# Decoder layer on one core: the first sequence's first two pairs staged, turned and reduced by halves of the tokens, beside the projections

## The reference

```python
qkv = x @ w_qkv
q, k, v = split(qkv)                      # 16 heads of 16
q = q * cos + rotate_half(q) * sin        # the same for k
att = where(causal, q @ k.T * scale, min)
y = softmax(att) @ v
x = layernorm(x + y @ w_proj)
x = layernorm(x + cross_attention(x, ctx))
x = layernorm(x + ffn(x))
```

## Time and profile before

| | us |
|---|---|
| median of 3 runs | 871.85 (871.64 to 872.28) |
| the profiled execution | 867.16 |
| its span, first to last instruction | 865.4 |
| TensorE busy | 803.2 (93%) |
| VectorE busy | 479.6 (55%) |
| ScalarE busy | 376.2 (43%) |
| GpSimd busy | 321.4 (37%) |

### The profile page before, as it was taken

The page is one execution under the profiler, slowest core; times in us unless marked ns, Lnnn a source line. Parts: engine busy times, 40 slices in busy tenths (PEclk is TensorE's granted clock), DMA queues, the critical chain, the costliest instruction groups (busy, mean ns, idle before and its releaser), DMA issues.

```text
span 865.4 us, 14094 instructions
## 1 busy us (share of the span) xinstructions
PE 803.2 (93%) x5044; PEld 542.1 (63%) x5044; DVE 479.6 (55%) x1257; ACT 376.2 (43%) x768; POOL 321.4 (37%) x585
## 2 busy tenths in 40 slices
PE   8879988898998999999999888989899899999996
PEld 4544444346776777877777634433577678887886
DVE  3797878536675542155444888871477661125113
ACT  0686776773444211223212377767544432113110
POOL 6313325245312543445332424323631143335433
PEclk9957999999999999999999999999999999999999
DMA  9900534430000232434332035510000000000000
GB/s 274 411 29 33 195 119 147 149 131 1 2 2 25 73 122 74 145 116 141 109 123 73 26 123 182 227 58 2 2 1 2 2 2 1 0 7 20 1 1 26
DMA packets 24712, 68.70 MB, mean 79 GB/s; under 512 B 4449, under 2 KB 11873, under 8 KB 24417
## 3 DMA queue, kind: packets, MB, share of 16 engines
q1 hardware_dynamic: 24640, 67.77, 22.4%
HBM read 65.40 MB, written 13.63 MB: 91 GB/s over the span
## 4 chain that ended last, share of the span: by engine, by line
PE 77%; DVE 10%; ACT 8%; issue 3%; POOL 2%; POOLq 0%; ACTq 0%; DVEq 0%
PE bank_pair L906 27%; PE bank_pair L729 7%; PE bank_pair L894 6%; PE bank_pair L711 6%; ACT prob_s L1048 5%; PE bank_pair L824 4%; PE bank_pair L615 3%; PE bank_pair L761 3%; PE bank_pair L675 3%; DVE bank_pair L1236 3%; PE bank_pair L659 3%; DVE max_raw L1234 3%; PE bank_pair L836 2%; PE bank_pair L903 2%; PE bank_pair L813 2%
## 5 line engine op out<-in xcount | busy, mean ns | idle before, releaser
L1539 POOL TENSOR_TENSOR hid_lo_s<-act_raw_s,hid_hi_s 128x512 fp32r<-128x512 f32 x96 | 124.5, 1298 | 175.4 <-DVE hid_hi_s L1383 136.4
L1048 ACT ACTIVATE prob_s<-bank_pair 128x512 f32<-128x512 f32 (+3 forms) x384 | 163.6, 505 | 57.0 <-PE bank_pair L711 56.5
L1236 DVE CUSTOM_DVE_ANT_0 bank_pair<-bank_pair,causal_bf 128x128 f32<-128x128 f32 (+3 forms) x256 | 120.2, 515 | 43.9 <-PE bank_pair L675 43.5
L675 PE MATMUL bank_pair<-k_t_s,q_t_s 64*128 64x512 f32 (+3 forms) x384 | 120.5, 439 | 3.2 <-DVE max_raw L1234 2.1
L711 PE MATMUL bank_pair<-q_t_s,k_t_s 64*128 64x512 f32 (+3 forms) x384 | 114.5, 409 | 8.4 <-ACT prob_s L1048 4.6
L1500 POOL TENSOR_SCALAR_AFFINE_SELECT prob_s<-prob_s 128x128 f32<-128x128 f32 x256 | 72.0, 295 | 132.1 <-ACT prob_s L1048 129.1
L1383 DVE CAST hid_hi_s<-act_raw_s 128x512 fp32r<-128x512 f32 x64 | 35.9, 565 | 144.8 <-ACT act_raw_s L1115 144.2
L1115 ACT ACTIVATE act_raw_s<-bank_pair,scales 128x512 f32<-128x512 f32 x64 | 42.9, 688 | 160.2 <-PE bank_pair L906 160.2
L711 PEld LDWEIGHTS bank_pair<-q_t_s,k_t_s 64*128 64x128 f32 x384 | 55.7, 190 | 90.5 <-ACT prob_s L1048 69.0
L906 PE MATMUL bank_pair<-hid_hi_s,home_s 128*128 128x512 f32 x256 | 99.8, 390 | 0.8 <-POOL hid_lo_s L1539 0.8
L906 PE MATMUL bank_pair<-hid_lo_s,home_s 128*128 128x512 f32 x256 | 99.6, 389 | 0.0
(11 more groups left out here) (157 smaller groups left out, 1422.3 us busy)
## 6 DMA issues: line engine op xcount, KB each, us to landing
ring_s<-scratch SPq DMA_DIRECT2D x34, 512.0 KB, 3.3
home_s<-scratch SPq DMA_DIRECT2D x22, 512.0 KB, 6.0
checked_s<-in_w_ffn SPq DMA_DIRECT2D x2, 3584.0 KB, 18.2
scratch<-in_w_ffn SPq DMA_DIRECT2D x2, 2560.0 KB, 10.1
ring_moved_s<-scratch SPq DMA_DIRECT2D x10, 512.0 KB, 3.3
checked_s<-in_w_ffn SPq DMA_DIRECT2D x1, 4096.0 KB, 32.4
x_t_s<-in_x_t SPq DMA_DIRECT2D x4, 512.0 KB, 4.2
x_tok_s<-in_x SPq DMA_DIRECT2D x2, 1024.0 KB, 9.1
```

The lines of the kernel that those rows point to most:

```text
L675: mm(out[:, 0:k1 - k0], qkt(q, p, 0)[r, P * qt:P * (qt + 1)], qkt(q, p, 1)[r, k0:k1], start=True, stop=True).then_inc(S["max_mm"], 1)
L1048: act.activation(prob[q][4 * (s % 2) + j][:, 0:n], score_bank(s, j)[:, 0:n], ACT.Exp, scale=SCALE).then_inc(S["exp_done"], 1)
L1236: dve.tensor_tensor_reduce(out=out[:, 0:left], in0=out[:, 0:left], in1=L["causal_bf"][:, CHUNK - left:CHUNK], scale=1.0, scalar=NEG, op0=A ...
L1539: pt(dst[1][:, m], act_raw[q][r % 3][:], dst[0][:, m].bitcast(F32), ALU.subtract).then_inc(S["f_lo"], 1)
```

## The change

For the first sequence, pairs 0 and 1 only, the stagings are cut into halves of the tokens, and a table of steps per sequence takes the place of the formulas. `Q_STEP` = -27 is the attention step that stands behind projection step t = 0, so t = 0 to 15 are also steps -27 to -12, and each engine's loop over projections calls `attention` behind each step. The lone steps begin at -11. In numbers of t:

| | pair 0 | pair 1 |
|---|---|---|
| staging, first half of tokens | 4 | 7 |
| turns i = 0, 1 | 6, 6 | 9, 9 |
| maxima, units 0 to 7 | 7, 8 | 10, 11 |
| staging, second half | 9 | 14 |
| turns i = 2, 3 | 12, 13 | steps -11, -10 |
| maxima, units 8 to 23 | steps -11 to -8 | steps -7 to -4 |

The units are numbered anew in the order in which they run (`UNIT_AT`), and the rounds too. The 16 early units go round two banks, 0 and 1, instead of six, since the other banks belong to projections and turns then; the first of them waits for the context's additions, which read these banks. The later 32 go round six. `stage_lo` of pair 0's first half stays with VectorE, the other halves' is GpSimd's. The 22 check pieces stand at two a step in steps -11 to -1. The second sequence keeps its steps.

```diff
-def stage_step(p):
-    return pair_base(p) - 13
+FIRST_STEP = (-11, pair_base(0) - 13)
+Q_STEP = FIRST_STEP[0] - (NT + V_LAG[0])
+STAGES = [[(Q_STEP + 4, 0, 0), (Q_STEP + 7, 1, 0), (Q_STEP + 9, 0, 1), (Q_STEP + 14, 1, 1)] +
+          [(pair_base(p) - 13, p, None) for p in range(2, NP)], [(pair_base(p) - 13, p, None) for p in range(NP)]]
...
+def turn_step(q, p, i):
+    if q == 0 and p < 2:
+        return ((Q_STEP + 6, Q_STEP + 6, Q_STEP + 12, Q_STEP + 13), (Q_STEP + 9, Q_STEP + 9, -11, -10))[p][i]
     return pair_base(p) - 12 + i
...
+def max_step(q, p, u):
+    if q == 0 and p < 2:
+        return Q_STEP + 7 + 3 * p + u // 4 if u < 8 else -11 + 4 * p + (u - 8) // 4
     return pair_base(p) - 8 + u // 4
...
 def check_step(n):
-    return FIRST_STEP + 4 + n * (-FIRST_STEP - 4) // PIECES
+    return FIRST_STEP[0] + n // 2
...
     def unit_bank(q, n):
+        if q == 0 and n < Q_UNITS:
+            return bank[n % 2]
         return bank[n % SHARED[q]] if n < FIRST_UNITS[q] else A_BANK[n % len(A_BANKS)]
     def units_ahead(q, n):
+        if q == 0 and n < Q_UNITS + SHARED[0]:
+            return 2 if n < Q_UNITS else 4
...
         def turn(q, p, i):
-            if i == 0:
-                wait(pe, q, "stage_hi", 2 * (p + 1))
-                wait(pe, q, "stage_lo", 2 * (p + 1))
+            if i % 2 == 0:
+                wait(pe, q, "stage_hi", stage_done(q, p, i // 2))
+                wait(pe, q, "stage_lo", stage_done(q, p, i // 2))
...
         def max_unit(q, p, u):
-            n = NU * p + u
+            n = UNIT_AT[q][p, u]
+            if n == 0:
+                wait(pe, q, "ctx_add", 2)
...
         for t in range(NT + V_LAG[0]):
             projections(0, t)
+            attention(0, Q_STEP + t)
         pe.wait_ge(w_in, 16 * 9)
-        for s in range(FIRST_STEP, S_END):
+        for s in range(FIRST_STEP[0], S_END):
             attention(0, s)
...
+        def stage_hi(q, n):
+            step, p, half = STAGES[q][n]
+            t0, t1 = (0, NT) if half is None else (NT // 2 * half, NT // 2 * (half + 1))
             if p == 0:
-                wait(dve, q, "rope_add", NT)
+                wait(dve, q, "rope_add", t1)
```

More of the change, by code:

```diff
@@ L119, with turns_done @@
 S_END = FINAL_STEP + 1
[L121 to L128 removed]
+ROUNDS = [[], []]
+for _q in range(BATCH):
+    for _s in range(Q_STEP, FINAL_STEP + 1):
+        ROUNDS[_q] += [("turn", p, i) for p in range(NP) for i in range(4) if turn_step(_q, p, i) == _s]
+        ROUNDS[_q] += [("rows", p, 0) for p in range(NP) if rows_step(_q, p) == _s]
+        ROUNDS[_q] += [("y", n, 0) for n in range(2 * NG) if y_step(n) == _s]
+        if _s == 0:
+            EARLY = len(ROUNDS[_q])
+ROUND_AT = [{r: n for n, r in enumerate(rounds)} for rounds in ROUNDS]
+assert ROUNDS[0][EARLY:] == ROUNDS[1][EARLY:]
+def turns_done(q, p, i):
+    return sum(r[0] == "turn" for r in ROUNDS[q][:ROUND_AT[q]["turn", p, i] + 1])
 XG = NG // 2
@@ L179 @@
 FLAG_BANK = 5
-FIRST_UNITS = (2 * NU, sum(max_step(p, u) < 0 for p in range(NP) for u in range(NU)))
+Q_UNITS = 16
+FIRST_UNITS = (2 * NU, sum(max_step(1, p, u) < 0 for p in range(NP) for u in range(NU)))
 SHARED = (6, 2)
@@ L480, in consumer @@
     def consumer(q, n):
-        kind = ROUNDS[n][0]
-        count = sum(r[0] == kind for r in ROUNDS[:n + 1])
+        kind = ROUNDS[q][n][0]
+        count = sum(r[0] == kind for r in ROUNDS[q][:n + 1])
         name = {"turn": "turn_evac", "rows": "rows_evac", "y": "y_norm"}[kind]
@@ L932, in attention @@
                 wait(pe, q, "ctx_add", 2)
-            units = [(p, u) for p in range(NP) for u in range(NU) if max_step(p, u) == s]
+            units = [(p, u) for p in range(NP) for u in range(NU) if max_step(q, p, u) == s]
             for j in range(4):
@@ L939, in attention @@
                     max_unit(q, *unit)
-                for kind, i, k in ROUNDS:
-                    if kind == "turn" and j == 1 and turn_step(i, k) == s:
+                for kind, i, k in ROUNDS[q]:
+                    if kind == "turn" and j == 1 and turn_step(q, i, k) == s:
                         turn(q, i, k)
-                    if kind == "rows" and j == 1 and rows_step(i) == s:
+                    if kind == "rows" and j == 1 and rows_step(q, i) == s:
                         rows(q, i)
@@ L1125, in attention @@
                 exps(q, s, (0, 1))
-            for kind, i, j in ROUNDS:
-                if kind == "turn" and turn_step(i, j) == s:
+            for kind, i, j in ROUNDS[q]:
+                if kind == "turn" and turn_step(q, i, j) == s:
                     turn_evac(q, i, j)
-                if kind == "rows" and rows_step(i) == s:
+                if kind == "rows" and rows_step(q, i) == s:
                     rows_evac(q, i)
@@ L1413, in attention @@
         def attention(q, s):
-            for p in range(NP):
-                if stage_step(p) == s:
-                    stage_hi(q, p)
+            for n, (step, p, half) in enumerate(STAGES[q]):
+                if step == s:
+                    stage_hi(q, n)
             for p in range(NP):
                 for u in range(NU):
-                    if max_step(p, u) == s:
+                    if max_step(q, p, u) == s:
                         reduce_unit(q, p, u)
-                if max_step(p, NU - 1) == s:
+                if max_step(q, p, NU - 1) == s:
                     join_max(q, p)
@@ L1451, in _ @@
         dve.wait_ge(set_pool, 11)
-        for t in range(NT):
-            projections(0, t)
-        for s in range(FIRST_STEP, S_END):
+        for t in range(NT + V_LAG[0]):
+            if t < NT:
+                projections(0, t)
+            attention(0, Q_STEP + t)
+        for s in range(FIRST_STEP[0], S_END):
             attention(0, s)
@@ L1556, in attention @@
         def attention(q, s):
-            for p in range(1, NP):
-                if stage_step(p) == s:
-                    stage_lo(q, p)
+            for n, (step, p, half) in enumerate(STAGES[q]):
+                if step == s and n:
+                    stage_lo(q, n)
             if 0 <= s < LAST:
@@ L1600, in _ @@
         fill(0)
-        for t in range(NT + 1):
-            projections(0, t)
-        for s in range(FIRST_STEP, S_END):
+        for t in range(NT + V_LAG[0]):
+            if t <= NT:
+                projections(0, t)
+            attention(0, Q_STEP + t)
+        for s in range(FIRST_STEP[0], S_END):
             attention(0, s)
```

90 lines of the change are left out of this document (42 added, 48 removed).

## The result

The changed kernel takes **878.89 us** (median of 5 runs, 878.46 to 882.82); the kernel before took 871.85 us in the median of 5 runs beside it (866.42 to 873.35). The two medians differ by 7.0 us. The ratio, which is estimated from all runs and is not the quotient of the two medians (that would be 1.0081), is 1.0104 with a 95% interval of 1.0071 to 1.0137, so the change costs 6.2 to 11.9 us. The prediction had 873.3, so the direction was right, and the growth by the medians was five times the +1.4 us of its sum. The profiled execution of the changed kernel took 878.89 us for a span of 877.2.

A forecast was written before the change was run, and what follows sets the result against it. VectorE and ScalarE, which empty TensorE's banks, were taken to bound the stage before the scores. The first exponential at 42.5 + 28.2 = 70.7, against 69.25, gave +1.4 us on the median 871.85: 873.3 us, range 869.3 to 879.5.

The forecast's parts named there:

- the +1.4 us of its sum: First exponential, end of the stage before the scores: forecast at 70.7 us against 69.25 before the change.
- Step (a): Lone steps: moving 16 of 48 maxima beside the projections cuts VectorE's 26.5 us there to 19.5, less some waits.
- Step (d): ScalarE behind the projections: busy without a hole for 28.2 us from 42.5, so the first exponential starts at 70.7.
- Step (b): Start of the first moved maximum, behind the last rope and pair 1's two half casts: 26.75 us.
- Step (c): Projections: v tiles queue behind early maxima, so the last v evacuation ends at about 41.4 instead of 31.75, 9.65 us growth.
- the hold: Projections: v tiles held up by VectorE's queue, laid out as 26.75 us and two blocks of 3.4.
- Step (e): Edits priced at nothing: bank numbers, wait counts, second sequence's tables; pair 1's transfer of rows is covered by the checks.
- the clock falls in the projections: TensorE goes to 1.2 GHz until the projections end: 881.2 us, or 877.3 if it returns halfway; chance 0.25.
- two of my own signs: Prediction called wrong if VectorE's join falls later than 63 us, or the granted clock before 41 us is below 1.0.
- faster by the plan: Projections: v tiles held up less; last v evacuation before 39.9 brings a gain, at 37.5 it is 869.4 us; chance 0.15.

The follow-up runs named there:

- a_cast: The changed kernel with the staging of pair 1's first half one projection step later, away from GpSimd's addition; 879.16 us, ratio 1.0112.
- a_warm: The changed kernel with 20 identity transposes, read by nothing, filling TensorE's gap between the second and third unit; 875.58 us, ratio 1.0067.
- a_banks: The changed kernel with four banks instead of two for the 16 early units; 873.65 us, ratio 1.0049.
- b_late: The kernel before, without the change, with 11 of its 22 check pieces moved to every fourth step with scores; 871.14 us, ratio 1.0005.
- a_late: The changed kernel with four banks for the early units and 11 check pieces at every fourth step with scores; 871.18 us, ratio 1.0005.
- b_fast: The kernel before with 11 late check pieces and two identity transposes ahead of each of its first 48 units; 894.17 us, ratio 1.0264.

## Why the prediction was right in direction and wrong in size

- **Step (a), what VectorE is spared: right.** It needed 26.5 us behind the projections and was to need 19.5; from its first maximum behind them (47.57) to the join (66.46) it takes 18.9. Step (d) had it done in 17.7 (42.1 to 59.8), and its own 16.8 us of maxima would make 58.9, so it was short there by over 1 us, which the sum doesn't use.
- **Step (b), the first moved maximum: 0.6 us short.** It was to start 2.15 us after the last rope's start (24.60 to 26.75) and starts 2.76 after it (25.20 to 27.96). I had shared one held cast of 0.90 among two half casts. The rule that I quoted from the Trainium skill, page "SBUF — State Buffer", section "Who interferes with whom", was right: this trace has 0.28 and 1.38 us side by side, and the 0.7 us more that I put beside the rule is near the 0.6 measured. With all that it drags along, `a_cast` puts the collision at 1.2 us.
- **Step (c), the projections: the step that failed.** Counted from the first rope, the last v evacuation was to end at 31.94 and ends at 36.90: 5.0 us late. 0.6 is the cast. Two things of (c) itself were wrong. The first is the 3.4 us from a pair's first maximum until TensorE is through with its eighth unit, for which I named the parts but gave no sum. It takes 4.5 us in pair 0 (27.96 to 32.47) and 4.1 in pair 1 (37.83 to 41.95), and 4.1 in both pairs of `a_warm`, where the clock stayed up. That is 0.7 twice, 1.4 us. With two banks VectorE and TensorE wait for each other in turn: VectorE stands idle before the fifth reading, until the products behind the v tile come, and TensorE before the seventh unit. For pair 1, DVE, then PE:

```profile
40.33 0.57 DVE L1275 CUSTOM_DVE_ANT_0 bank_pair<-bank_pair,causal_bf 128x384 f32<-128x384 f32 x1 [0.80 <-PE bank_pair L710]
...
41.01 1.00 PE L710 MATMUL bank_pair<-k_t_s,q_t_s 64*128 64x512 f32 x2 [0.71 <-DVE max_raw L1275]
```

  The second is the clock, which (c) leaves at its upper level: v tile 1 takes 2.07, two turns 1.06 each, v tile 2 1.49. `a_warm` measured this term by itself: 2.6, of which 0.4 lies in pair 0's 4.5. The remaining 0.4 is spread over the turns and v tiles behind. Without the hold (`a_banks`) the last v ends at 29.8, and all of the 7.0 us are gone.
- **Step (d), ScalarE without a hole: right.** Its first turn evacuation follows the last v evacuation by 1.28 us (1.1), and the first exponential follows that by 28.61 us (28.2), with no wait between. (That nearly all of ScalarE's other time before the change was waits for turns misreads: its 3.7 us begin at 32 us, ahead of the first check. Between 34.90 and 69.25 the waits for turns are 2.9 us, and another 1.9 are for the rows of maxima. The sum doesn't use it.) VectorE's join lies 10.4 us ahead of the first exponential. The two terms add 0.6, and 1.4 + 5.0 + 0.6 = 7.0.
- **Step (e): nothing showed there.** No transfer of rows ends a wait of the stage.
- **The rival "the clock falls in the projections" came true in part.** I gave it 0.25 and a time of 877.3 to 881.2. By two of my own signs the forecast was wrong: the granted clock is below 1.0 before 41 us, and VectorE's join, at 66.46, falls later than 63. The last v evacuation, at 46.96, is where this rival had it, too. But the clock was down for only some 7 us, so it cost 2.6, not 4 to 8; that 878.89 still lies within the rival's 877.3 to 881.2 is luck, since the hand-overs and the cast added the rest. The Trainium skill, page "TensorE: Matmul & The Clock Gate", section "A second HAM failure mode: psum-queue depth-cycling", spoke against the change, and the trace agrees in half: 0.53 amid the hand-overs of pair 0 (30 to 33 us), and 1.00 amid those of pair 1 (39 to 42 us), which are of the same form.
- **The rival "faster by the plan" had its point right.** It was to decide with the last v evacuation before 39.9, or 39.3 with the 0.6 us of step (d); in `a_banks` it ends at 39.74, 39.24 if 0.5 for the later first rope is taken off, and the first exponential is level with before.

## What to carry to other kernels

Work that is moved beside another stage takes that stage's queue with it: if it gets only the banks that happen to be free, a product of the other stage stands behind each reading of it. So the sum must count round trips, and the number of banks comes before the question of whose engine is free. Where two engines end a stage within 1 us of each other, as `b_late` showed, taking 7 us off one of them alone can bring 1 us at most; look for that first. When two variants are compared, see that the same piece of work stands last in both: one check of 1.05 us ahead of the first exponential hid the 0.6 us that `a_late` had won at its first score. And an idle engine is only usable in slices as long as the piece: a check of 1.0 to 1.2 us between evacuations of 0.38 made the products wait.

## What was not expected of the hardware

- The first cast of two ran free (0.28 us) and the second for 1.38 us, until GpSimd's addition was over; the same happened at 18.45 us, where the 2.08 us hole hid it.
- The clock is not a property of the program alone. With the same instructions in the projections it stayed at 1.00 in the profile of `a_banks` and fell to 0.81 and 0.62 in that of `a_late`. In `b_fast` it fell with TensorE busy for 2.63 of the 3 us ahead.
- The start of the first rope moved between 8.91 and 10.06 us from run to run, as the first loads landed, and took the whole stage with it: 1.1 us, as much as the smaller effects looked for here.
